# The Silu of a convolution, written as a tanh on ScalarE and one VectorE instruction

## What is computed

```python
rn = resid * rsqrt(mean(resid * resid) + EPS) * norm_w
skip = rn @ skip_w.T
x_in = rn @ in_w.T                                   # 512 channels
conv = conv_b + sum(xp[:, k:k + L, :] * conv_w[:, k] for k in range(4))
x = silu(conv)                                       # the line that changes
delta = softplus(x @ wd1.T @ wd2.T + wd2_b)
Bm, Cm = x @ wB.T, x @ wC.T
h = exp(delta * A) * h + (delta * x) * Bm            # step by step, 16 states a channel
y = (sum over states of h * Cm + x * W_D) * silu(skip)
out = resid + y @ out_w.T
```

## Time and profile before

| | us |
|---|---|
| median of 3 runs | 1269.93 |
| the profiled execution, its own time | 1272.05 |
| span of its instructions | 1270.2 |
| VectorE busy | 1173.1 (92%) |
| TensorE busy | 1076.9 (85%) |
| ScalarE busy | 1010.5 (80%) |
| GpSimd busy | 998.2 (79%) |

### The profile page before, as it was taken

How to read it: one execution, slowest core, us unless ns; L and a number is a source line. 1 busy time by engine, 2 the same in 40 slices (tenths; PEclk the granted TensorE clock), 3 DMA queues, 4 the chain that set the end, 5 groups by cost and what they waited for, 6 DMA issues and landing times.

```text
span 1270.2 us, 20047 instructions
## 1 busy us (share of the span) xinstructions
PE 1076.9 (85%) x5406; PEld 806.6 (64%) x5406; DVE 1173.1 (92%) x2128; ACT 1010.5 (80%) x2151; POOL 998.2 (79%) x601
## 2 busy tenths in 40 slices
PE   4378576498898989999999999999999999998776
PEld 3266475365666666676767766676766667675664
DVE  5976899989999899999999999999999999999896
ACT  4898346379888897889888898889889898987853
POOL 1487176667898988889898998889899898988764
PEclk8686778798999999999999999999999999998977
DMA  7467822644445454555545454555545455544536
GB/s 229 154 200 227 312 82 82 203 162 130 142 141 153 135 148 153 145 149 137 149 133 161 134 161 139 147 148 131 155 139 157 142 150 150 147 134 132 135 128 191
DMA packets 87117, 195.08 MB, mean 154 GB/s; under 512 B 11184, under 2 KB 47152, under 8 KB 86928
## 3 DMA queue, kind: packets, MB, share of 16 engines
q1 hardware_dynamic: 69008, 171.18, 40.7%
q0 software_dynamic: 17712, 22.55, 10.9%
q10 hardware_dynamic: 288, 0.07, 0.0%
HBM read 171.22 MB, written 26.48 MB: 156 GB/s over the span
## 4 chain that ended last, share of the span: by engine, by line
PE 31%; POOL 29%; ACT 14%; issue 13%; DVE 11%; DMA 1%; POOLq 0%; DVEq 0%; ACTq 0%
POOL part L775 15%; PE yps L870 7%; POOL acc L831 5%; POOL tap L805 4%; ACT aexp L557 4%; PE bankX L1067 4%; PE bankH L1033 4%; PE bankV L1057 4%; DVE hb L1170 3%; PE bankG L910 3%; POOL scr L783 2%; ACT L557 2%; DVE bps L1149 2%; PE bankV L910 2%; POOL x L807 2%
## 5 line engine op out<-in xcount | busy, mean ns | idle before, releaser
L775 POOL TENSOR_TENSOR part<-hb,bcr 128x1024 f32<-128x1024 f32 x256 | 618.3, 2429 | 172.4 <-DVE hb L1170 141.2
L1170 DVE TENSOR_TENSOR_SCAN hb<-aexp,carry,bps 128x256 f32<-128x256 f32 x768 | 545.5, 734 | 4.2 <-ACT aexp L557 4.1
L557 ACT ACTIVATE aexp<-delta,Am 128x256 f32<-128x256 f32 x1024 | 446.8, 501 | 53.0 <-DVE hb L1170 42.0
L870 PE MATMUL yps<-idn,part 128*128 128x128 f32 x2048 | 299.8, 286 | 74.1 <-POOL part L775 64.0
L1149 DVE TENSOR_TENSOR bps<-ups,bcr 128x512 f32<-128x512 f32 x512 | 345.8, 675 | 3.4 <-DMA bcr<-brows 2.3
L870 PEld LDWEIGHTS yps<-idn,part 128*128 128x128 f32 x2048 | 249.9, 147 | 151.2 <-POOL part L775 83.0
L1170 DVE TENSOR_TENSOR_SCAN hb<-aexp,bps 128x256 f32<-128x256 f32 x256 | 167.3, 673 | 10.8 <-ACT aexp L557 10.2
L1067 PE MATMUL bankX<-w,scr 128*128 x568 | 138.7, 388 | 10.5 <-ACT scr L715 8.1
L1033 PE MATMUL bankH<-w,scr 128*128 x284 | 136.8, 604 | 2.2 <-issue 1.0
L1057 PE MATMUL bankV<-v,scr 128*128 x284 | 134.2, 595 | 1.2 <-ACT xin L610 0.8
L831 POOL DMA_INDIRECT acc<-scr,idx x71 | 114.2, 1609 | 24.6 <-issue 11.5
(11 more groups left out here) (179 smaller groups left out, 1625.1 us busy)
## 6 DMA issues: line engine op xcount, KB each, us to landing
bcr<-brows SPq DMA_DIRECT2D x256, 512.0 KB
w<-in_W SPq DMA_DIRECT2D x2, 4096.0 KB, 22.1
xch<-in_x SPq DMA_DIRECT2D x16, 256.0 KB, 4.5
w<-in_x SPq DMA_DIRECT2D x4, 1024.0 KB, 9.7
xt<-scr SPq DMA_DIRECT2D x16, 256.0 KB, 3.0
acc<-scr SPq DMA_DIRECT2D x16, 256.0 KB, 2.8
v<-in_V SPq DMA_DIRECT2D x1, 4096.0 KB, 16.0
acc<-mst POOLq DMA_DIRECT2D x15, 256.0 KB
```

The source lines that it names most:

```text
L557: nc.scalar.activation(aexp[:, w % EXP_SLOTS, i, :], delta[:, c % 2, e, :], ACT.Exp, scale=Am[:, e, n:n + 1]).then_inc(s_a, 1)
L775: nc.gpsimd.tensor_tensor(part[:, slot:slot + 2, :, :], hb[:, state:state + 2, :, :], bcr[:, row:row + 2, CH:2 * CH].unsqueeze(2).to_broad ...
L870: mm = pe.matmul(yps[:, s, i * P:(i + 1) * P], part[:, w % (2 * PART_PAIRS), i, s * P:(s + 1) * P], idn[:, :], start=(n == 0 and s == 0 an ...
L1170: v.tensor_tensor_scan(hb[:, w % STATE_SLOTS, i, :], aexp[:, w % EXP_SLOTS, i, :], bps[w % 2][:, i, :], first, ALU.mult, ALU.add).then_inc ...
```

## The change

On ACT the Silu in place becomes a Tanh of x2 into `tap`, all four blocks at once; on DVE a new piece X2 waits for it and writes (tap + 1) * x2 back into x2; it is DVE that raises x2r now. DVE's X2 stands two units after the place in the table. So that the convolution gives half the sum, DVE halves its weights `cw` and its bias `cb` once, ahead of everything that uses them.

```diff
 LATER = {
     ...
-    "DVE": {"FA": 1, "FB": 1, "X2": 5, "O1": 1, "O2": 4, "DL": 5},
+    "DVE": {"FA": 1, "FB": 1, "X2": 2, "O1": 1, "O2": 4, "DL": 5},
...
                 elif kind == "CV" and piece[2] not in DVE_CONV:
                     e, c = piece[1], piece[2]
+                    act.wait_ge(half_set, 2)
                     act.wait_ge(conv, KE * c + e)
...
                 elif kind == "X2":
                     c = piece[2]
                     act.wait_ge(conv, KE * (c + 1))
-                    nc.scalar.activation(x2[:, c % 2, :, :], x2[:, c % 2, :, :], ACT.Silu).then_inc(x2r, 1)
+                    at_least(act, brow_w, 32 * c)
+                    nc.scalar.activation(tap[:, :, :], x2[:, c % 2, :, :], ACT.Tanh).then_inc(x2t, 1)
...
+                elif kind == "X2":
+                    c = piece[2]
+                    dve.wait_ge(x2t, c + 1)
+                    v.scalar_tensor_tensor(out=x2[:, c % 2, :, :], in0=tap[:, :, :], scalar=1.0, in1=x2[:, c % 2, :, :],
+                                           op0=ALU.add, op1=ALU.mult).then_inc(x2r, 1)
...
             dve.wait_ge(ld_first, 16 * FIRST_LOADS)
+            v.tensor_scalar(cw[:, :, :], cw[:, :, :], 0.5, None, ALU.mult).then_inc(half_set, 1)
+            v.tensor_scalar(cb[:, :], cb[:, :], 0.5, None, ALU.mult).then_inc(half_set, 1)
+            dve.wait_ge(half_set, 2)
             for piece in prologue():
                 do(piece)
```

More of the change, by code:

```diff
@@ L352, in mamba_moe @@
         cvd = sem("cvd")
+        x2t = sem("x2t")
+        half_set = sem("half_set")
         x2r = sem("x2r")
```

## The result

| | before | after |
|---|---|---|
| median, us | 1270.06 (4 runs) | 1299.78 (4 runs, 1297.78 to 1302.2) |
| ratio | 1 | 1.0228, 95% interval 1.0213 to 1.0242 |
| profiled execution, us | 1272.05, span 1270.2 | 1298.72, span 1296.9 |
| VectorE (DVE) busy, us | 1173.1 | 1212.9 |
| ScalarE (ACT) busy, us | 1010.5 | 969.1 |

The kernel is 29.7 us slower; I had 1274.6, in a range from 1267.3 to 1281. The busy times are to be read against what was forecast: ACT lost 41.4 us, just the forecast 41, but DVE got 39.8 us fuller for one instruction a chunk that I had put at 1.2 us, 19 in all. First the groups of instructions of the kernel after that stand where the removed loads and the row of the price stood: line, engine, operation, tiles, shapes and count, busy us and mean ns of one, idle before.

The account below looks back on a forecast made before the run. DVE was taken as the fullest engine, PE close behind. Prologue +2.35, chunk 0 -0.85, chunk 1 +1.13, chunks 2 to 14 (-0.3 + 1.9 + 0.2 + 0.3) gave +4.7 on 1269.93: 1274.6 us, range 1267.3 to 1281.

Parts of the forecast that it names:

- What it adds: On DVE, one scalar_tensor_tensor over 128 x 1024 per chunk at 1.13 us, ends 1.0 and 1.3; halvings cost nothing.
- That cover is 0.2 us: In chunk 7, PE's convolution product, now waiting for DVE, has 0.2 us cover; an instruction of 1.4 makes PE late.
- The loads: On ACT, table loads go from 104 to 72, none at the activation; busy time falls by 41 us.
- The wait of 1.98 at 85.83: In chunk 0, DVE's wait for ACT vanishes and takes in the instruction, so DVE gains 0.85 us.
- the moments start at 24.66: In the prologue, DVE's first moments start at 24.6 instead of 22.24, adding 2.35 us.
- The chunk-by-chunk sum: Chunks 2 to 14: 0.63 each for X2 of chunks 6, 10, 13; under 0.1 for four others; whole sum +4.7.
- a four-chunk period off by over 1 us: Sign of being wrong: time between ends of two four-chunk periods, 289 us, moves by over 1 us either way.
- A: Rival: the instruction is taken in nearly everywhere by DVE's waits; +1.8, 1271.7 us; chance 0.26.
- C: Rival: full price, DVE at 98% passes everything on through POOL and PE; +13, 1283 us; chance 0.13.
- D: Rival: slow instruction, two float32 tensors read at half pace, 2.2 us each; +17, 1287 us; chance 0.03.
- E: Rival: the tanh needs table loads of its own, so no wait comes back; +10.7, 1280.6 us; chance 0.02.
- B: Rival: faster, expert tiles' tanh comes earlier on ACT, 0.4 gained in each of 13 chunks; -2.6, 1267.3 us; chance 0.14.

Follow-up runs that it names:

- e2: Kernel before plus one unused scalar_tensor_tensor per chunk on DVE, second input in PSUM, nothing waiting for it: 1273.41 us, ratio 1.002.
- e5: Kernel before with Tanh in place of Silu on ACT and nothing added on DVE, multiplication left out: 1263.7 us, ratio 0.9944.
- e12: Kernel before with the edits of e5 and e2 together, multiplication left out: 1269.38 us, ratio 0.9992.
- e7: Changed kernel with tanh in PSUM for seven chunks and the first three X2 kept as Silu on ACT: 1275.68 us, ratio 1.004.
- e4: Changed kernel with a sigmoid in place of the tanh, which brings the table loads back: 1303.4 us, ratio 1.0248.

## Why the prediction was wrong

**The step that failed** is the first of "What it adds": one instruction a chunk at 1.13 us, between ends of 1.0 and 1.3. It takes 1.2 us when it meets no GpSimd product or comes ahead of one, 1.3 to 2.3 in three cases, and 3.57 to 3.84 in half of the chunks; the mean is 2.54. Both durations that I went by the earlier trace rows were measured under the favourable condition: the 424 ns with GpSimd idle, and in the 1215 of L1282 DVE had always begun before GpSimd. A price was read, but not what stood beside it. All the other DVE work around X2 runs beside GpSimd's products undisturbed; its second input comes from PSUM (the scans' `bps`, the products' `ups`), as in e2, and this made GpSimd look harmless.

The trace of before had the sign. The views of two other lines of DVE, in the router and in the convolution, show instructions of one shape that differ by a factor of two, and the timeline shows one of them against a GpSimd product:

```profile
L1279 DVE TENSOR_TENSOR w<-w x8: 719/1000/1391, 157.5 to 225.2; 128x568 f32<-128x568 f32 x8
...
L1294 DVE TENSOR_SCALAR x<-xin,cw,cb x8: 408/600/931, 14.7 to 202.8; 128x256 f32<-128x256 f32 x8
...
211.04 2.35 POOL L775 TENSOR_TENSOR part<-hb,bcr 128x1024 f32<-128x1024 f32 x1 [1.47 <-DVE hb L1170]
212.75 1.25 DVE L1279 TENSOR_TENSOR w<-w 128x568 f32<-128x568 f32 x1
```

The last ends at 214.00, 0.6 us after GpSimd's at 213.39, and it takes 0.72 to 0.75 where no GpSimd product is beside it. The forecast read the mean of groups; the smallest and the largest of the line would have told.

**The second step that failed** hangs on the first: "That cover is 0.2 us: if the instruction takes 1.4, PE is late too." The bound was right and the instruction passed it. PE waits 2.3 us in each of the seven chunks, 20.6 us in ten waits, where I had called more than one or two a sign of being wrong. That TensorE's clock falls behind such a wait stood nowhere in the forecast.

**What was right.** The loads: 104 to 72, none at the activation, ACT lighter by 41.4. The wait of 1.98 at 85.83 is gone, and the moments start at 24.66 (forecast 24.6):

```profile
23.52 1.22 DVE L1314 SCALAR_TENSOR_TENSOR x<-tap,x 128x1024 f32<-128x1024 f32 x1 [1.12 <-ACT tap L628]
24.66 0.42 DVE L1112 BATCH_NORM_STATS2 st<-w 128x6 f32<-128x256 f32 x1
```

The chunk-by-chunk sum for an instruction that costs 1.13: with the stop taken away (tanh in PSUM, seven), chunks 6, 10 and 13 step by 0.6, for which 0.63 was put, and chunks 7, 8, 11 and 12 by 0.5, 0, 0.5 and -0.2, for which under 0.1 each was put. The profiled execution's sum was forecast at +4.7 and is +4.7, but that agreement is luck: this kernel's median is 9.5 over before, as its profiled execution was the fastest of its six runs, and chunks 0 to 3 differ from the forecast by up to 2.5 both ways (chunk 0 was put at -0.85 and is +1.6). So even with the seven stops taken away the forecast is about 5 us too low. The condition that I had set for being wrong, a four-chunk period off by over 1 us, is met by far: chunks 8 to 11 together are 8.6 us longer.

**The rivals.** A, that the instruction is taken in, is what happens to one without a stop: 15 x 1.18 us cost 2.2 us. C, the full price, fails by the same run. D, half pace, would have given 1287 and was the nearest number, for a wrong reason. By the Trainium skill, "Vector Engine (DVE) Microarchitecture Reference", section "Points that are easy to get wrong", the form with two sources in SBUF that aren't bfloat16 halves its throughput; here 1024 columns take 1.197 to 1.224 us wherever GpSimd is out of the way, and the same form with one source in PSUM 1.18 for 1008, so the trace doesn't show it. I had weighed the Trainium skill's rule about the pace of this form and missed the one about the neighbour, in "SBUF — State Buffer". E is excluded by the loads. B's gain of 0.4 in a chunk where an expert tile follows isn't seen: the change made in three of them alone gains nothing that can be told (1.0003).

**The sum of the 29.7 us.** By differences of medians: the stop in the seven chunks with PE's wait and the lower clock beside it, 20.1 (change against PSUM in seven); the prologue and chunks 0 and 1, 4.0 (against Silu kept there); what is left, 5.5 to 5.6, is the cost of the remaining instructions less what the loads give back. That last part isn't taken apart further: the two halves measured alone (e2 and e5, and both in e12) give -1.7, and e7 gives +5.5 over before with three instructions fewer. These some 7 us can lie in B3 and the exponentials hanging on DVE, in the stops outside the seven chunks (3.57 us in chunk 2, 1.72 in chunk 4, 2.27 in chunk 14), and in the loads that e7 keeps (chunk 0 steps by 1.7 there and by -1.5 in e12); which of them wasn't tried. At B3 itself e7's PE waits for DVE only once, 0.55 us. That chunk 2's stop is cheap, since an expert tile is due there for whose tanh DVE waits anyway, as in the earlier trace rows, is argued and not shown.

## What to carry to other kernels

Before an instruction is put on VectorE, look where its inputs lie and what GpSimd runs at that moment: with two inputs in SBUF (or as a float32 `tensor_scalar` from SBUF to SBUF) it may wait for the rest of GpSimd's instruction and the whole of the next one, so that its price here was between 1.2 and 3.8 us by its neighbour alone. Take a price not from the mean of a group but from its smallest and largest, and say for the row what the other engines did beside it. And a relief of an engine that isn't the bound is worth what the bound waits for it, here 6.5 of 41 us, which leaves little room for any instruction on the full engine.

## What the runs showed of the hardware that was not expected

- In the seven chunks of the change a second GpSimd product, back to back with the first, goes ahead of a DVE instruction that began to wait in the last 0.2 to 0.4 us of the first (591.50 to 595.11 against products that end at 594.03). The longest stop, 2.6 us, is so a little over one product. In chunk 14 the instruction came earlier, 1.19 us before the first product's end, and there it went ahead of the second:

```profile
1197.52 5.64 POOL L779 TENSOR_TENSOR part<-hb,bcr 128x1024 f32<-128x1024 f32 x2
1198.68 2.27 DVE L1314 SCALAR_TENSOR_TENSOR x<-tap,x 128x1024 f32<-128x1024 f32 x1
```

- What GpSimd runs first need not be a product. In the eighth long case, chunk 2, only an indirect DMA was running when the instruction came, with 0.10 us to go, and the product behind it still went first:

```profile
299.45 1.01 POOL L787 DMA_INDIRECT scr<-xt,idx  x1
300.36 3.57 DVE L1314 SCALAR_TENSOR_TENSOR x<-tap,x 128x1024 f32<-128x1024 f32 x1
300.48 2.36 POOL L779 TENSOR_TENSOR part<-hb,bcr 128x1024 f32<-128x1024 f32 x1
```

- DVE ends 1.08 to 1.09 us after GpSimd, and not 1.2: about 0.1 us of an instruction's 1.2 is done or hidden while it stands.
- GpSimd's indirect DMA (L835) is itself held by this DVE instruction. Where it begins while DVE's instruction runs or stands, it ends 1.45 to 1.49 us after DVE's, every time, and takes 2.4 to 2.6 us in place of 1.60; beside the instruction with one input in PSUM (e2) it stays at 1.6. Where it had begun 0.4 us ahead (e4, 377.28), neither is held: 1.58 and 1.23 us.

```profile
516.33 1.20 DVE L1314 SCALAR_TENSOR_TENSOR x<-tap,x 128x1024 f32<-128x1024 f32 x1
516.42 2.57 POOL L835 DMA_INDIRECT acc<-scr,idx  x1 [0.16 <-issue]
```

- Where DVE is first, GpSimd's product is longer by 0.9 (3.23 against 2.36), less than the 1.03 that was left of DVE's instruction.
- A table load costs ACT its 1.283 us and no more: the load of the earlier trace rows starts with no idle time ahead of it. The absence of 32 is worth 6.5 us of the kernel's time.
- DVE, at 98% in the middle of the run, took in 17.8 us of new work for 2.2 us of time.
- "Busy" counts the stop: DVE is shown as 39.8 us fuller, of which some 21 (40.6 - 16 x 1.2) is standing still.
